# Sort stage of a four-layer graph network: steps by groups of four chunks, bias seeded by ScalarE, one key comparison

## The reference, cut to what matters

```python
# second layer
gate = jax.nn.sigmoid(jax.nn.silu(rbf @ W1 + b1) @ W2 + b2)   # rbf = edge_attr_64 (50000, 64)
msg  = gate * h[src]
aggr = jax.ops.segment_sum(msg, dst, num_segments=h.shape[0])
```

## Time and profile before

| | us |
|---|---|
| median of 3 runs (4747.5 to 4752.62) | 4750.72 |
| span of the profiled execution, first to last instruction | 4744.9 |
| the loop of lines 575 to 739 within the span | about 172 to 778 |

### The profile page before, as it was taken

How to read it: one execution, slowest core, us unless ns; L and a number is a source line. 1 busy time by engine, 2 the same in 40 slices (tenths; PEclk the granted TensorE clock), 3 DMA queues, 4 the chain that set the end, 5 groups by cost and what they waited for, 6 DMA issues and landing times. The chain is left out here.

```text
span 4744.9 us, 105920 instructions
## 1 busy us (share of the span) xinstructions
PE 3915.0 (83%) x22300; PEld 3233.3 (68%) x22301; DVE 3382.7 (71%) x9318; ACT 1791.0 (38%) x5399; POOL 3071.7 (65%) x3178
## 2 busy tenths in 40 slices
PE   6799997889987889878899566779978778578886
PEld 3477775778776778767777556668866666366664
DVE  7799997667757778677787667874257778756666
ACT  0355553221123333333333100004257667367774
POOL 0266665777756777567775777766777773067774
PEclk9799998999998999989999777888978898778787
DMA  1233334856626445264452687861465444144445
GB/s 47 92 131 131 130 132 130 212 126 158 152 63 202 135 145 154 71 185 146 145 149 78 208 257 214 245 191 54 145 182 120 105 106 125 32 99 109 109 109 100
DMA packets 643665, 643.00 MB, mean 136 GB/s; under 512 B 314342, under 2 KB 549540, under 8 KB 643396
## 3 DMA queue, kind: packets, MB, share of 16 engines
q0 software_dynamic: 145840, 374.54, 27.8%
q1 hardware_dynamic: 443348, 213.36, 17.0%
q10 hardware_dynamic: 54336, 53.65, 3.3%
HBM read 470.09 MB, written 170.26 MB: 135 GB/s over the span
## 5 line engine op out<-in xcount | busy, mean ns | idle before, releaser
L1059 POOL DMA_INDIRECT G<-h_dram,idx x1572 | 1525.8, 971 | 556.8 <-issue 361.6
L1283 PEld LDWEIGHTS ps_a<-hotm,msg 128*128 128x128 f32 x4716 | 686.5, 193 | 196.2 <-DVE arena L1395 67.5
L1283 PE MATMUL ps_a<-hotm,msg 128*128 128x128 f32 x4716 | 730.0, 282 | 88.5 <-DVE arena L1395 87.8
L1271 PE MATMUL ps_e<-nnw,attT 128*128 128x256 f32 x2358 | 738.4, 396 | 76.8 <-DVE prodm L1388 42.4
L1395 DVE TENSOR_TENSOR arena<-ps_a,arena 128x256 f32 x1404 | 586.9, 418 | 218.8 <-issue 94.1
L735 POOL DMA_INDIRECT rec_dram<-rec,pos x392 | 376.7, 961 | 398.6 <-ACT rec L606 307.7
L1059 POOL DMA_INDIRECT G<-feat_dram,idx x420 | 402.4, 958 | 325.5 <-POOLq L241 197.9
L1317 ACT ACTIVATE msg<-prodm 128x256 f32<-128x256 f32 x786 | 327.5, 417 | 677.8 <-DVE prodm L1388 586.1
L749 POOL DMA_INDIRECT rec_dram<-rows,place x392 | 379.8, 969 | 222.1 <-issue 117.4
L1897 POOL DMA_INDIRECT arena<-rel_dram,idx x393 | 385.0, 980 | 128.6 <-issue 86.2
L1271 PEld LDWEIGHTS ps_e<-nnw,attT 128*128 128x128 f32 x2358 | 370.3, 195 | 118.4 <-DVE prodm L1388 56.4
(11 more groups left out here) (365 smaller groups left out, 7691.6 us busy)
## 6 DMA issues: line engine op xcount, KB each, us to landing
gate<-rec_dram SPq DMA_DIRECT2D x126, 384.0 KB
G<-msg_dram SPq DMA_DIRECT2D x300, 128.0 KB, 2.2
msg_dram<-msg ACTq DMA_DIRECT2D x270, 128.0 KB
rel_dram<-stage SPq DMA_DIRECT2D x25, 1040.0 KB
G<-h_dram,idx POOLq DMA_INDIRECT x1572
aT<-edge_attr SPq DMA_DIRECT2D x98, 128.0 KB
msg_dram<-arena ACTq DMA_DIRECT2D x90, 128.0 KB
attT<-attT_dram SPq DMA_DIRECT2D x74, 144.0 KB
```

What stands on the lines that cost most here:

```text
L1059: pool.indirect_dma_start(G[:, n % width, :], None, table, bass.IndirectOffsetOnAxis(ap=idx[:, which, n:n + 1], axis=0)).then_inc(sem(f"sw ...
L1271: t.matmul(ps_e[s % BANKS][:], attT[:, s // HU, s % HU, :], nnw[:], start=True, stop=True).then_inc(sem("ew"), 1)
L1283: last = t.matmul(ps_a[s % BANKS][:, h, :], of[:, h * P:(h + 1) * P], hot[:, s, :], start=True, stop=True)
```

## The change

The loop steps by groups instead of pairs: two steps for two groups (`width=2`), and the second layer lags by one group. In a step for group g, PE runs the counts before (was line 655), W1 for all four chunks of g (was line 635), W2 for the four chunks of g-1 in two halves q (was line 645, each half ends with its own `g`), and the rest of the counts (was line 661). DVE runs the comparison of g, the silu of g-1, and then the look-ups, sums, wait and metadata of g in one go. Silu and sigmoid take 512 columns at once instead of 256. Line 641 is gone: ACT copies b2, loaded into all partitions, into each half of `ps_g`, once ahead of the loop and then after each gate (`seeded`), and PE's W2 matmuls add to it. Two matmuls of zeros ahead of the loop prime the two banks. The comparisons of lines 469 and 471 become one over 400 columns, from a table `keys4` that is built ahead. The sum for line 719 goes to `pos_s`, and the places of the second order are written once, after the loop. `sig` and `silu` move into the arena.

```diff
@@ setup
-                        for q in range(3):
-                            sp.dma_start(b2[32 * q:32 * q + 1, :], ...).then_inc(sem("w_in"), 16)
+                        sp.dma_start(b2[:], L1_gnn_b2.rearrange("(a d) -> a d", a=1).to_broadcast([P, D])).then_inc(sem("w_in"), 16)
...
+                        v.tensor_copy(keys4[:, :, 0:R3], key_d.unsqueeze(2).to_broadcast([P, EC, R3]))
+                        v.tensor_copy(keys4[:, :, R3], key_s)
...
-                        for q in range(3):
-                            step(v.tensor_copy(b2part[:], b2[:] if q == 0 else b2rest[:]))
-                            v.tensor_copy(b2b[32 * q:32 * q + 1, :], b2part[32 * q:32 * q + 1, :])
-                            step(v.tensor_tensor(b2rest[:], b2[:] if q == 0 else b2rest[:], b2part[:], ALU.subtract))
@@ one_hot_keys
-                    nc.vector.tensor_tensor(OK[:, b, :, 0:KD], ..., ALU.is_equal)
-                    return nc.vector.tensor_tensor(OK[:, b, :, KD:K], ..., ALU.is_equal)
+                    return nc.vector.tensor_tensor(
+                        OK[:, b, :, :].rearrange("p j (f k) -> p j f k", f=R3 + 1),
+                        keys4[:, ds(g * SG, SG), :].unsqueeze(3).to_broadcast([P, SG, R3 + 1, KS]),
+                        iota[:, 0:K].rearrange("p (f k) -> p f k", f=R3 + 1).unsqueeze(1).to_broadcast([P, SG, R3 + 1, KS]),
+                        ALU.is_equal)
@@ ACT
+                        act.wait_ge(sem("primed"), 1)
+                        for q in range(2):
+                            nc.scalar.copy(ps_g[q][:], bias2).then_inc(sem("seeded"), 1)
+                        for c0, c1 in walk(nc.scalar, NG // 2, 0, 1, width=2):
+                            if c0:
+                                g, i, b = c0
+                                act.wait_ge(sem("z"), upto(g))
+                                act.wait_ge(sem("silu"), upto(g - 2))
+                                for h in range(DH):
+                                    last = nc.scalar.activation(by_pairs(sig, b, h), first_layer(b, h), ACT.Sigmoid, bias=b1[:, h:h + 1])
+                                last.then_inc(sem("sig"), 1)
                             if c1:
+                                g, i, b = c1
+                                for q in range(2):
+                                    act.wait_ge(sem("g"), g * 2 + q + 1 + CREDIT)
+                                    if not isinstance(i, int) or i > 0:
+                                        for j in range(2):
+                                            act.wait_ge(sem(f"sw_rec{b * SG + 2 * q + j}"), i * OUTS)
+                                    nc.scalar.activation(rec[:, b, 2 * q:2 * q + 2, 0:D], ps_g[q][:], ACT.Sigmoid).then_inc(sem("gate"), 1)
+                                    act.wait_ge(sem("gate"), g * 2 + q + 1 + CREDIT)
+                                    nc.scalar.copy(ps_g[q][:], bias2).then_inc(sem("seeded"), 1)
...
@@ PE
+                        for q in range(2):
+                            last = t.matmul(ps_g[q][:].rearrange("p j d -> p (j d)"), zerob[:],
+                                            identb[:].unsqueeze(1).to_broadcast([P, SG, P]), start=True, stop=True)
+                        last.then_inc(sem("primed"), 1)
...
+                            if c0:
+                                g, i, b = c0
+                                pe.wait_ge(sem("hot"), g + 1)
+                                for j in range(SG - 1):
+                                    last = t.matmul(ps_r[:, j + 1:SG, :], identb[:], four(OK[:, b, j, :], SG - 1 - j), ...)
+                                last.then_inc(sem("before"), 1)
+                                pe.wait_ge(sem(f"attr_in{b}"), i * 32 + 32)
+                                pe.wait_ge(sem("silu"), upto(g - 2))
+                                for q in range(2):
+                                    for h in range(DH):
+                                        for j in range(2):
...
+                                            last = t.matmul(ps_z[b][:, j, at:at + P], W1[rows, h * P:(h + 1) * P],
+                                                            aT[rows, b, q, :], start=True, stop=True)
+                                last.then_inc(sem("z"), 1)
                             if c1:
-                                t.matmul(ps_g[s % 2][:], onesb[:], b2b[:].unsqueeze(1).to_broadcast([b2b.shape[0], 2, D]), start=True, stop=True)
+                                g, i, b = c1
+                                pe.wait_ge(sem("silu"), upto(g))
+                                for q in range(2):
+                                    pe.wait_ge(sem("seeded"), g * 2 + q + 1)
                                     for j in range(2):
+                                        for h in range(DH):
+                                            last = t.matmul(ps_g[q][:, j, :], silu[:, b, h, 2 * j + q, :], W2[:, h, :], start=False,
+                                                            stop=(h == DH - 1), skip_group_check=True)
+                                    last.then_inc(sem("g"), 1)
                             if c0:
+                                pe.wait_ge(sem("looked_up"), g + 1)
+                                for j in range(SG):
+                                    last = t.matmul(ps_r[:, 0:j + 1, :], identb[:], four(OK[:, b, j, :], j + 1), ...)
+                                last.then_inc(sem("counted"), 1)
@@ DVE
+                            if c0:
+                                g, i, b = c0
+                                dve.wait_ge(sem("counted"), g + 1)
+                                one_hot_keys(g, b).then_inc(sem("hot"), 1)
                             if c1:
+                                g, i, b = c1
+                                dve.wait_ge(sem("sig"), upto(g))
+                                dve.wait_ge(sem("g"), (g - 1) * 2 + CREDIT)
                                 for h in range(DH):
+                                    last = v.scalar_tensor_tensor(by_pairs(silu, b, h), first_layer(b, h), b1[:, h:h + 1],
+                                                                  by_pairs(sig, b, h), ALU.add, ALU.mult)
                                 last.then_inc(sem("silu"), 1)
                             if c0:
...
+                                dve.wait_ge(sem("summed"), g + 1)
+                                if not isinstance(i, int):
+                                    for j in range(SG):
+                                        dve.wait_ge(sem(f"sw_rec{b * SG + j}"), i * OUTS)
...
+                        dve.wait_ge(sem("placed"), NG)
+                        v.tensor_tensor(place2[:], pos_s, trash2, ALU.add)
```

More of the change, by code:

```diff
@@ L297, in sort_edges @@
                 tmp_i = area(4 * EC).bitcast(I32).rearrange("p (f c) -> p f c", f=4)
+                keys4 = area(4 * EC).rearrange("p (c f) -> p c f", f=4)
                 key_d, key_s = area(EC), area(EC)
+                pos_s = area(EC)
                 trash1, trash2 = area(EC), area(EC)
@@ L336, in sort_edges @@
                 b2 = sb(ctx, "b2", [P, D])
[L337 to L340, removed]
                 b1 = sb(ctx, "b1", [P, DH])
                 aT = sb(ctx, "aT", [P, 2, SG // 2, P])
-                sig = sb(ctx, "sig", [P, 2, DH, 2, P])
-                silu = sb(ctx, "silu", [P, 2, DH, 2, P])
+                sig, silu = (area(2 * DH * SG * P).rearrange("p (b h s e) -> p b h s e", b=2, h=DH, s=SG) for _ in range(2))
                 pctx = ExitStack()
@@ L386, in _ @@
                         sp.wait_ge(sem("x_in"), 32)
[L387 removed]
+                        sp.wait_ge(sem("w_in"), 16 * 6)
                     @block.gpsimd
@@ L573, in sort_edges, with first_layer, by_pairs @@
                 ps_z = [ps(pctx, f"ps_z{b}", [P, 2, 512]) for b in range(2)]
-                ps_g = [ps(pctx, f"ps_g{b}", [P, 2, D]) for b in range(2)]
+                ps_g = [ps(pctx, f"ps_g{q}", [P, 2, D]) for q in range(2)]
+                def first_layer(b, h):
+                    return ps_z[b][:].rearrange("p j (q h e) -> p j q h e", q=2, h=DH)[:, :, :, h, :]
+                def by_pairs(of, b, h):
+                    return of[:, b, h, :, :].rearrange("p (j q) e -> p j q e", j=2)
                 with nc.Block() as block:
@@ L588, in _ @@
                         credit(act, "a32", "sig", "gate")
-                        for c0, c1, c2 in walk(nc.scalar, NG // 2, 0, 1, 2, width=PAIRS):
-                            if c1:
[L591 to L608, removed]
-                                b = s // 2
@@ new lines, in _ @@
+                                dve.wait_ge(sem("hot"), g + 1)
+                                dve.wait_ge(sem("before"), g + 1)
+                                left = ps_r[:, :, 0:KD]
+                                v.tensor_tensor(prod[:, b, :, KD:K], ps_r[:, :, KD:K], OK[:, b, :, KD:K], ALU.mult)
```

(11 more changed lines are left out.)

114 lines of the change are left out of this document (22 added, 92 removed).

## The result

The changed kernel takes 4837.38 us (median of 4 runs, 4834.88 to 4841.81), the kernel before, on the same chip, 4751.67 us (4 runs). The ratio is 1.0181 (95% interval 1.0167 to 1.0196), so the change costs some 86 us. The forecast was 4792, at most 4837: right side, right place, but only half the size. The number given for "PE loses its clock" was 4837; as will be seen, that agreement is partly luck.

What follows compares the result with a forecast made beforehand. Bound: a closed chain over two groups, through scatters freeing record buffers. (12.95 - 12.16) x 48 = 38 us, plus 3 for late scatters, gives 41 on 4750.7: 4792 us; own range 4769 to 4823, 8-in-10 range 4745 to 4837.

Steps and rivals of the forecast that it cites:

- PE loses its clock: Rival: PE pauses some 0.8 us per group, matmuls run at clock 0.78, chain 13.90 us, time 4837 us; chance 0.13.
- line 711 waits over 1 us in each group: Sign on DVE: line 715's successor waits for the sort stage's scatters, over 1 us in each group.
- The sum of the chain: Closed loop over two groups, from line 715 through the scatters to line 715 again: 12.95 us, bounds 12.58 to 13.48.
- metadata to record: Chain term on DVE, line 715 to line 721: 0.41 us.
- to the comparison: Chain term on DVE, from line 721 to the comparison: 0.29 us.
- PE to the start of W2: Chain term on PE: hand-over 0.10, counts before 0.35, W1 of four chunks 2 x 0.64; 1.73 us, bounds 1.63 and 1.84.
- W2 to the gate: Chain term, W2's first half on PE until ACT's gate: 2.00 us, from rows of 2.07 and 1.93.
- fourth scatter to line 711: Chain term, from the fourth scatter's start until the metadata line (then 715) may go: 2.77 us, bound 2.71.
- a granted clock of the stage visibly below 1.00: Sign in the profile after: if the stage's clock falls so, the prediction's size is wrong.
- late scatter: Scatter idle 2.16 us where 0.30 is usual, costing up to 1.86 in a tight chain; 3 us added for three (0 to 6).
- Start and end: Priming PE and W1 before the first W2, against savings in the last group: together 0, between -2 and +3 us.
- PE sets the pace: Rival: the chain is shorter than 11.24 us, a group takes 5.62 us, -45 us, time 4706 us; chance 0.12.

Runs made afterwards that it cites:

- e1_seven_buffers: The changed kernel with seven buffers of rec and pos in place of two, order kept, loop written out over 14 groups: 4715.82 us, ratio 0.9934.
- e3_late_metadata: The changed kernel with DVE's wait for scatters and the metadata behind it moved to the end of the next group's step, two buffers kept: 4694.53 us, ratio 0.9891.
- e4_filler: The changed kernel with four more matmuls of 512 columns per group on PE, into a bank nobody reads, ahead of PE's pause: 4817.16 us, ratio 1.0144.
- e7_twice_compared: The changed kernel with DVE making each comparison of 400 columns twice, first into a scratch area: 4864.13 us, ratio 1.0261.
- e2_pairs_seeded: The kernel before, its steps by pairs kept, with ACT's seeds of b2 instead of bias matmuls and one comparison per group: 4744.96 us, ratio 1.0001.

## Why the prediction was right in kind and wrong in size

**What bounds the changed loop.** As put: DVE waits for the scatters of the group two back, PE for DVE. Shown by the trace, and by e1_seven_buffers and e3_late_metadata, each of which takes the wait away in its own manner and with it the whole loss. That line 711 waits over 1 us in each group was wrong: the two groups take turns, one waits 2 us and one not at all.

**The sum of the chain: 12.95 put, 13.28 measured** (round of 407.73). Term by term:

| term | put | measured |
|---|---|---|
| metadata to record (711 to 716) | 0.41 | 0.51 |
| to the comparison | 0.29 | 0.54 |
| comparison of 400 columns | 0.58 | 0.58 |
| PE to the start of W2 | 1.73 | 1.51 |
| W2 to the gate | 2.00 | 2.16 |
| gate | 0.60 | 0.60 |
| to the first scatter | 0.76 | 0.77 |
| three more scatters | 3.81 | 3.80 |
| fourth scatter to line 711 | 2.77 | 2.81 |

The sum lies within the bounds that were put, 12.58 to 13.48. Most rows of before carried over. Two terms came out longer, by 0.10 (metadata to record) and by 0.16 (W2 to the gate), for which no run was made. "To the comparison" was read in the middle of a turn of the loop; in the waiting group the loop's turn stands there, 0.35 us marked issue. W1 of four chunks was put at twice the 0.64 of two, 1.28, and takes 1.10 (409.77 to 410.87), which gave 0.18 back. The error of 0.33 is 16 us in 48 rounds. So at full clock the loop should have grown by (13.28 - 12.16) x 48 = 54 us, where 38 was put. e4_filler, at nearly full clock, is near that: 13.41 a round are 60 us in 48 rounds, and 0.0144 of 4750 are 68 us for the whole kernel, with what lies outside the rounds.

The Trainium skill (DMA: Bandwidth & Descriptors, section on the anatomy of one DMA on the gpsimd path) gives a fixed cost of about 2.0 us, by which alone the chain would have been about as long as two groups of before (12.18 against 12.16). The section adds a part for the bytes at 436 GB/s, which the prediction left out: an estimate by that figure for the 150 KB of one scatter is 0.34 us more, a chain of 12.52, and some 17 us for the change. The trace has 2.81 from the scatter's start to the engine that it wakes, and the row decided rightly.

**The step that failed: the lower clock as a case apart.** The prediction put the lower clock at nothing in its sum. It gave "PE loses its clock" a chance of 0.13 and took it for all 48 rounds or for none, from a pause of 0.8 us in every group. In fact PE's pause gathers in every second group, 2.16 us, and the clock falls in 12 of 48 rounds: they exceed 13.28 us by 18.6 us together. It belonged into the sum, as a part of the rounds at a price of some 1.5 us each. That the clock is the cause of these long rounds, and not a part of the chain, is shown by their granted clock and by e4_filler: with PE kept busy most of them went, while the wait for scatters stayed. The prediction had named the sign, a granted clock of the stage visibly below 1.00, and it is 0.97.

With the chain's 16 us these are about the 34 us by which the loop outgrew its forecast (75.2 against 38 and 3). The chain's error alone would have left the time within the forecast's own range (up to 4823); the clock and what lies outside the loop carried it out. The two long rounds at nearly full clock exceed 13.28 us by 3.7 together; the one of 734.85 (1.8 of it) has a late scatter as the prediction had added 3 us for, and that term holds.

The rival's 13.90 a round lies near the measured mean of 13.78 (rounds counted from 186.24), and its 4837 on the median, but by luck: it took the lower clock for all matmuls of a chain of 12.95, where the runs show a longer chain and a few long rounds.

**Start, end and the rest.** The first scatter comes 5.0 us later. Of that, 2.35 is the setup, which the prediction put at 0: the loop's first comparison starts at 174.09 instead of 171.74. No run shows which part of the setup grew. The other 2.6 are the start of the loop, and its end gives 1.0 back: the last group takes 9.48 us from line 711 (847.74) to its last scatter, the round shown 10.47. Start and end together are within the bound that was put (-2 to +3).

Behind the loop, where no code differs, the profiled execution is 9.1 us longer; by the medians, which differ by 85.7, about 5.5. The three kernels with the closed chain (this one, e4_filler, e7_twice_compared) take 3977 to 3979 us there in their profiled executions, the other six 3967 to 3970 (before: 3968). So it hardly is chance, but no run was made for it, and the cause stays open.

**The rival "PE sets the pace".** It fell as a forecast, but its number tells what the change is worth when nothing holds it up: 5.62 us a group put, 5.43 measured in e3_late_metadata. The bias matmuls gave less than put (0.32, not 0.46). W1's 16 matmuls in one row gave 0.18 that was not put, and the counts after 0.09, since they take 0.44 in e3_late_metadata (410.62 to 411.06) and took 0.53 before:

```profile
403.97 0.59 PE L661 MATMUL ps_r<-OK,identb 128*128 128x100 bf16 x4
404.50 0.71 PE L635 MATMUL ps_z<-aT,W 64*128 64x128 f32 x8
```

The steps by four did one more thing that the prediction did not see: they take away the loop between DVE and PE that held the old order at 6.01 (e2_pairs_seeded).

## What to carry to other kernels

A wait for a buffer to come free is a closed chain: add up all that lies from it round to itself, and compare with buffers times the time of a step; an order that puts the release behind more work can make a slack chain the bound without any engine doing more. When it does, look where in each engine's queue the wait stands, and move it behind the work that others wait for, before adding buffers (0.9891 against 0.9934 here, where the body written out for seven buffers also cost some 15 us of pauses). And when a forecast turns an engine from always busy to pausing, put the pause where it will gather (one long one, not several short ones) and cost the clock for a part of the rounds.

## What the runs showed of the hardware

- After the pause of 2.16 us of PE that ended at 256.42 the granted clock was 0.84 (254 to 260) and 0.81 (260 to 264); after the equally long one that ended at 409.41 it was 1.00 (407 to 414), with the same work around it. The runs don't show what decides between them. With four extra matmuls of 512 columns in each group the stage was granted 1.00.
- PE's time is not the sum of its rows: a bias matmul of 0.23 us costs 0.16 net (0.32 for two), since the half of W2 behind it gets 0.06 shorter.
- The turn of a loop costs DVE 0.35 us where the body has two groups, and about 3 us where it has fourteen.
